# A fused two-layer cross-attention kernel: where text is scaled, where a weight is loaded, who splits what

## The chip, the cores and the metric

The kernel runs on one core of one Trainium2 chip. The metric is device time in microseconds (us) of one execution. The engines are TensorE (PE in the profile, with its weight loads as PEld), VectorE (DVE), ScalarE (ACT), GpSimd (POOL) and SyncE (SP, which here issues DMAs only). ACT issues DMAs too; in the profile SP's hardware DMA queue is q1 and ACT's is q10.

## The reference, cut to what matters

Two attention layers run one after the other on `x` (8 x 100 x 640), with the same context `ctx` (8 x 722 x 1024), of which the first 77 tokens are text and the other 645 are called ip. There are 20 heads of 32.

```
layer 1: q = x Wq.T; k,v = text Wk.T, Wv.T; k_ip,v_ip = ip Wk_ip.T, Wv_ip.T
         out = (softmax(q k /sqrt(32)) v + softmax(q k_ip /sqrt(32)) v_ip) Wo.T + bo + x
layer 2: the same with its own weights, and for the ip part
         tp    = softmax((q k_text) /sqrt(32))       # over all 640 channels at once
         sem   = ((tp text) ip.T) /sqrt(32)
         ip_p  = softmax(q_h k_ip_h /sqrt(32) + 0.5 sem) * mask
         out = (softmax(..) v + ip_p v_ip) Wout + bout + x
```

## The kernel before, in words

**Numbers.** The large products are made of float16 pairs: each operand is scaled by a power of two, rounded to float16 (the high part, on ACT) and its rest is rounded again (the low part, on DVE or POOL). A product is three matmuls per slice of the contraction (`pairs`, L510: high-high, high-low, low-high). The scale comes from the largest absolute value of the whole operand: DVE reduces each partition (`text_part` L1381, `weight_part` L1344, `context_part` L1393, `q_part` L1450), PE turns the column of 128 maxima into a row (`turn`, L530), and DVE reduces that row and makes the scale in four one-column instructions (`turned_max` L1326, `scale_chain` L1331 to L1338).

**Order.** Nothing is scheduled by a program: every engine has its own list, written out by hand, and waits on semaphores. Each layer has a prologue, and then 40 windows (8 batch rows times 5 groups of 4 heads). The prologue goes through query tiles (`q_tile`, L477, float32), the text keys (`kt_unit`, five units of 48 matmuls), the text values (`vt_unit`, five units), the ip keys of the first two groups (`k_part`), the odd tokens (`odd_unit`), and the first ip values (`v_tile`). In layer two the text logits and the semantic term of row 0 come between them. Products go to two PSUM banks in turn. A bank is free again once ACT has written the high part (L950 for keys, L961 for values) and DVE the low part (L1418, L1432).

**Text and weights in layer one.** Text lies in eight slices `k`. ACT writes the high part of each (`split_text`, L912). The even slices get their low part on DVE (`text_low`, L1387); the odd ones are first multiplied by the scale on POOL (`scale_text`, L1214) and then subtracted on POOL (`split_text`, L1220). `kt_unit(0, 0)` waits for all eight slices and for the four weight quarters, whose high parts ACT writes (`split_weight`, L900) and whose low parts DVE writes (`weight_low`, L1366).

**Buffers that tie engines to DMAs.** The high and low text keys of unit g lie in one of two buffers, and SP stores each unit with two DMAs to `k_dram` (L427). `kt_unit(l, g)` on ACT waits, for g of 2 and more, until the stores of unit g-2 have landed. It is the same with the text values (`vt_unit`, SP's L432), two buffers and one DMA each. After the last of them SP loads `sel`, stores and reloads the queries (`place_q`: L327, L330), and stores and reloads the ip keys of a group (`place_k`: L337, L341). `k_unit` (ACT L980, DVE L1507) writes the one buffer from which L337 stores, so it waits for the store of the group before. `odd_unit` on PE waits for both halves of the second `k_unit` pair.

**Weights and context in layer two.** The fourth weight (the ip values' one) comes in four quarters of 640 KB on ACT's queue (`load_weight(1, 3)`, L889), each of which waits for a low part of the third weight. The split context rows 0 and 1 are read back from `c_dram` in one DMA of 2580 KB each (`fetch_context`, L925); row 1 overwrites the buffer in which the fourth weight's quarters lie, and so waits for that weight's low parts. DVE takes the maxima of the quarters (`weight_parts`, `weight_max` L1352), and PE turns them (`weight_turn(1, 3)`) between two text value units.

**Chores in a window.** In layer one, while row i is worked on, the context of row i+1 is split during the windows of g = 1 and g = 2. POOL's part of it (`scale_context` L1227 and `split_context` L1233 of the odd slices) is hung behind its three `prob_low` instructions (L1257) per window, which PE waits for before `weigh` (L658). PE's order at the end of a window is `max_scores` of head 0 (L611), a piece of `k_part`, `weigh(u, 3)`, `max_scores` of head 1, and so on; `max_scores` of a head waits until DVE has read the row of the head before (`maxima`, L1524 and L1532).

Of the kernel before, what the change touches and what calls it, by code (L numbers as in the profile page):

```python
# [23 lines left out]
KT = CC // P  # L24
CT = C // P
# [4 lines left out]
TT = 5  # L30
# [29 lines left out]
VA = 3  # L60
ADDED = (1, 3, 5)
SLICES = (0, 2, 1, 3, 4, 6, 5, 7)

# [6 lines left out]
def xattn_pair_kernel(nc, ctx_d, text_d, x_d, w_d, wq_d, wo_d, bias_d, mask_d, const_d, sel_d, kd, qd, vd, cd, out_d):  # L70
    with ExitStack() as stack:
# [248 lines left out]
        def _(sp):  # L320
# [97 lines left out]
            sp.dma_start(x_late, x_d[1]).then_inc(x_in[1], 16)  # L418
            for s in t_low:
                sp.wait_ge(s, KT // 2)  # L420
            for h in range(2):
# [49 lines left out]
        def _(pe):  # L471
# [63 lines left out]
            def kt_unit(l, g):  # L535

                if g == 0:
                    pe.wait_ge(w_low, 16 * l + 4)
                    if l == 0:
                        for s in t_low:  # L540
                            pe.wait_ge(s, KT // 2)
                for c in range(2):
                    bank, full = bank_ready(pe, "kt", l, g, c)
                    a = ODDS + c * 4 * TEXT
                    pairs(bank[:, 0:4 * TEXT], text_weights(0, g * P, (g + 1) * P), texts(a, a + 4 * TEXT)
                          ).then_inc(full, 1)

            def vt_unit(l, t):

                if t == 0:  # L550
                    pe.wait_ge(w_low, 16 * l + 8)
                for c in range(2):
                    bank, full = bank_ready(pe, "vt", l, t, c)
                    a = ODDS + t * P
                    b = min(a + P, TW)
                    pairs(bank[0:b - a, 0:C // 2], texts(a, b), text_weights(1, c * C // 2, (c + 1) * C // 2)
                          ).then_inc(full, 1)
# [238 lines left out]
            weight_turn(0, 0)  # L796
            q_tile(0, 1, 1)
            turn(ts, t_chain, 1, "text")
            for c in range(2, CT):
                q_tile(0, 1, c)  # L800
# [44 lines left out]
            turn(qs, q_chain, 6, "q", 1)  # L845
            kt_unit(1, 4), vt_unit(1, 0), vt_unit(1, 1)
            weight_turn(1, 3)
            vt_unit(1, 2), vt_unit(1, 3), vt_unit(1, 4)
            for c in range(2):
# [31 lines left out]
        def _(act):  # L881
# [26 lines left out]
            def split_text(k):  # L908

                if k % 2:  # L910
                    act.wait_ge(t_scaled, k // 2 + 1)
                nc.scalar.activation(t_hl[:, 0, k, :], text_raw[:, k, :], ACT.Copy,  # L912
                                     scale=1.0 if k % 2 else ts[:, 4:5]).then_inc(t_high, 1)

# [238 lines left out]
            kt_unit(1, 2)  # L1153
            split_weight(1, 2, (2, 3))
            load_weight(1, 3)
            kt_unit(1, 3), kt_unit(1, 4)
            fetch_context(0)
            vt_unit(1, 0), vt_unit(1, 1)
            split_weight(1, 3, (0, 1))
            vt_unit(1, 2)  # L1160
            split_weight(1, 3, (2, 3))
            vt_unit(1, 3)
            act.wait_ge(w_low, 32)
            fetch_context(1)
            vt_unit(1, 4)
            for c in range(2):
# [3 lines left out]
            act.wait_ge(vt_out[0], 96)  # L1170
            k_unit(STEPS, 0), k_unit(STEPS, 1)
            logits(0)
            k_unit(STEPS + 1, 0), k_unit(STEPS + 1, 1)
# [12 lines left out]
        def _(pool):  # L1186
# [73 lines left out]
            def window(l, i, g):  # L1260
# [7 lines left out]
                if l == 0 and i < B - 1 and g == 1:  # L1268
                    chores = iter((lambda: (scale_context(r + 1, 3), split_context(r + 1, 1)),
                                   lambda: split_context(r + 1, 3)))  # L1270
# [23 lines left out]
            pool.wait_ge(t_chain, 5)  # L1294
            for k in range(1, KT, 2):
                scale_text(k)
            for k in range(1, KT, 2):
                split_text(k)
# [23 lines left out]
        def _(dve):  # L1322
# [427 lines left out]
            weight_scale(0, 0)  # L1750
            weight_lows(0, 0, (0, 1))
            turned_max(ts, "text")
            scale_chain(ts, t_chain, 0, ts[:, 4:5], ts[:, 5:6])
            weight_lows(0, 0, (2, 3))
            for k in range(0, KT, 2):
                text_low(k)
            weight_parts(0, 1, range(4))
            weight_max(0, 1)
            for c in range(CT):
                q_part(0, 0, c)  # L1760
            kt_unit(0, 0)
# [8 lines left out]
            weight_max(0, 2)  # L1770
            for c in range(CT):
                q_part(0, 1, c)
            q_max(0)
            kt_unit(0, 4)
            weight_scale(0, 2)
# [60 lines left out]
            kt_unit(1, 3)  # L1836
            q_scale(1)
            weight_parts(1, 3, (0, 1))
            kt_unit(1, 4)
            weight_parts(1, 3, (2, 3))  # L1840
            vt_unit(1, 0)
            weight_max(1, 3)
            weight_scale(1, 3)
            vt_unit(1, 1)
            weight_lows(1, 3, (0, 1))
            vt_unit(1, 2)
            weight_lows(1, 3, (2, 3))
            vt_unit(1, 3)
            layer_scale(1)
            vt_unit(1, 4)  # L1850
            q_split(B)
            new_scale(B)
# [73 lines left out]
```

## Time and profile before

| | us |
|---|---|
| median of 3 runs | 1921.87 (1921.60 to 1924.43) |
| the profiled execution | 1930.09 |
| its span in the profile | 1928.3 |
| PE busy | 1833.7 (95%) |
| DVE busy | 1164.6 (60%) |
| ACT busy | 781.8 (41%) |
| POOL busy | 430.7 (22%) |
| PEclk, all 40 slices | 9 tenths or more of full speed |

The span is cut into 40 slices of some 48 us. PE's busy row reads `7889999999999999998978999999999999999998`: below 9 are the prologue of layer one (slices 1 to 3), the turn to layer two and its prologue (slices 19, 21 and 22) and the end. A PE that is counted busy can still be at half its clock, since TensorE has two levels of it, 1.2 and 2.4 GHz.

### The profile page before, as it was taken

Reading aid. Unit: us, or ns where it says so; the run is one execution under the profiler, and the core shown is the slowest. Engines: PE = TensorE matmul, PEld = TensorE weight load, DVE = VectorE, ACT = ScalarE, POOL = GpSimd, SP = SyncE. Lnnn points to the kernel's source line nnn. Section 1 sums busy time; section 2 is a strip of 40 time slices with the busy share of each in tenths; the row PEclk is TensorE's granted clock in tenths of the full one; section 3 lists DMA queues with packets and bytes.
Section 4 is the critical chain, followed back from the end, with each engine's and each line's share of the span. In section 5 each row is a group of like instructions: output and inputs, shape, how many; then the busy total and the mean of one; then the engine's idle time right before and its main releaser. Section 6 shows DMA issues by size and latency. Waiting matters only on the chain.

```text
span 1928.3 us, 53974 instructions
## 1 busy us (share of the span) xinstructions
PE 1833.7 (95%) x23163; PEld 1463.6 (76%) x23163; DVE 1164.6 (60%) x2904; ACT 781.8 (41%) x1569; POOL 430.7 (22%) x522
## 2 busy tenths in 40 slices
PE   7889999999999999998978999999999999999998
PEld 4567888888888788884556788878787877878874
DVE  5776666767676767546442556566565656565653
ACT  3243454455454545442221334344343433343441
POOL 3132342423242424221000112121121112121120
PEclk9999999999999999999999999999999999999999
DMA  5753344343344343443084122323131413232221
GB/s 242 150 169 84 117 136 123 124 129 116 111 127 120 105 143 97 132 146 136 13 153 140 26 54 83 91 69 106 48 106 41 126 48 104 58 112 55 82 54 43
DMA packets 122311, 198.49 MB, mean 103 GB/s; under 512 B 40424, under 2 KB 109432, under 8 KB 115480
## 3 DMA queue, kind: packets, MB, share of 16 engines
q1 hardware_dynamic: 116600, 164.50, 30.6%
q10 hardware_dynamic: 5472, 30.54, 4.4%
q8 instruction: 183, 3.00, 0.7%
q14 instruction: 56, 0.46, 0.1%
HBM read 133.91 MB, written 60.88 MB: 101 GB/s over the span
## 4 chain that ended last, share of the span: by engine, by line
PE 77%; DVE 8%; DMA 7%; ACT 4%; issue 2%; POOL 2%; SPq 0%; ACTq 0%; POOLq 0%; DVEq 0%
PE proj L510 50%; PE pv L658 5%; PE proj L477 5%; PE rows L611 4%; PE st L634 3%; PE rows L510 3%; DMA k_dram<-arena 3%; DMA arena<-k_dram 2%; PE st L642 2%; PE rows L612 2%; ACT arena L1005 1%; DMA cbuf<-w_dram 1%; DVE wparts L1344 1%; PE rows L620 1%; DVE w_hl L1366 1%
## 5 line engine op out<-in xcount | busy, mean ns | idle before, releaser
L510 PE MATMUL proj<-w_hl,cbuf 128*128 128x128 f16 x9600 | 602.0, 219 | 0.7 <-issue 0.7
L510 PE MATMUL proj<-cbuf,w_hl 128*128 128x322 f16 (+1 forms) x3840 | 595.1, 301 | 5.0 <-DVE arena L1507 2.6
L510 PEld LDWEIGHTS proj<-w_hl,cbuf 128*128 128x128 f16 x9600 | 549.2, 98 | 7.8 <-issue 1.3
L510 PEld LDWEIGHTS proj<-cbuf,w_hl 128*128 128x128 f16 x3840 | 369.7, 97 | 171.8 <-DVE arena L1507 2.9
L1257 POOL TENSOR_TENSOR arena<-arena 128x400 f16<-128x400 f32 x240 | 235.1, 979 | 937.3 <-ACT arena L1005 937.3
L1004 ACT ACTIVATE arena<-st,rs 128x400 f16<-128x400 f32 x480 | 287.0, 598 | 373.6 <-PE st L642 159.5
L1005 ACT ACTIVATE arena<-st,rs 128x400 f32<-128x400 f32 x480 | 285.6, 595 | 0.0
L980 ACT ACTIVATE arena<-proj 128x323 f16<-128x323 f32 (+1 forms) x160 | 70.5, 442 | 502.7 <-PE proj L510 489.0
L1552 DVE TENSOR_TENSOR arena<-arena 128x400 f16<-128x400 f32 x240 | 146.2, 609 | 139.7 <-ACT arena L1005 132.0
L658 PEld LDWEIGHTS pv<-arena 128*128 128x128 f16 x4480 | 184.6, 97 | 48.2 <-POOL arena L1257 13.2
L658 PE MATMUL pv<-arena 128*128 128x66 f16 (+1 forms) x4480 | 199.0, 185 | 11.7 <-POOL arena L1257 8.2
L634 PE MATMUL st<-arena 128*128 128x100 f16 x1920 | 163.1, 207 | 0.8 <-ACT arena L1005 0.5
L1647 DVE TENSOR_TENSOR st<-st,sem_t 128x400 f32<-128x400 f32 x120 | 69.9, 582 | 152.5 <-PE st L634 152.1
L1524 DVE TENSOR_REDUCE mx<-rows 100x1 f32<-100x77 f32 x320 | 75.4, 236 | 131.1 <-PE rows L612 130.9
L611 PE MATMUL rows<-arena 96*128 96x512 f16 x320 | 122.0, 381 | 17.8 <-DVE mx L1528 11.6
L1528 DVE CUSTOM_DVE_ANT_0 raw<-rows,raw 100x645 bf16<-100x645 f32 x160 | 131.6, 822 | 0.0
L1532 DVE TENSOR_REDUCE mx<-rows 100x1 f32<-100x645 f32 x160 | 131.1, 819 | 0.0
L1507 DVE SCALAR_TENSOR_TENSOR arena<-proj,arena 128x323 f16<-128x323 f32 (+1 forms) x160 | 78.9, 494 | 75.7 <-ACT arena L980 73.3
L634 PEld LDWEIGHTS st<-arena 128*128 128x128 f16 x1920 | 114.3, 98 | 3.3 <-issue 1.2
L612 PE MATMUL rows<-arena 96*128 96x229 f16 x320 | 84.0, 263 | 0.0
L510 PE MATMUL proj<-arena,t_hl 128*128 128x320 f16 (+1 forms) x480 | 67.3, 303 | 11.3 <-DVE arena L1418 9.4
L1517 DVE SCALAR_TENSOR_TENSOR arena<-proj,arena 128x384 f16<-128x384 f32 (+1 forms) x160 | 77.2, 483 | 1.2 <-ACT arena L988 1.1
(166 smaller groups left out, 1793.8 us busy)
## 6 DMA issues: line engine op xcount, KB each, us to landing
arena<-k_dram SPq DMA_DIRECT2D x240, 185.2 KB, 3.6
k_dram<-arena SPq DMA_DIRECT2D x80, 322.5 KB, 2.9
c_dram<-cbuf SPq DMA_DIRECT2D x16, 1290.0 KB, 6.9
raw<-ctx_dram SPq DMA_DIRECT2D x14, 1290.0 KB, 7.7
cbuf<-c_dram SPq DMA_DIRECT2D x12, 1290.0 KB
cbuf<-w_dram ACTq DMA_DIRECT2D x24, 640.0 KB, 6.7
arena<-q_dram SPq DMA_DIRECT2D x48, 125.0 KB, 2.6
cbuf<-c_dram ACTq DMA_DIRECT2D x2, 2580.0 KB
```

What stands on the lines that cost most here:

```text
L477: mm = nc.tensor.matmul(bank[:, 0:MT], weight[:, c, k], src[:, k], start=(k == 0), stop=(k == CT - 1))
L510: mm = nc.tensor.matmul(out, x[a](k), w[b](k), start=(k == 0 and m == 0), stop=(k == KT - 1 and m == 2))
L611: nc.tensor.matmul(rows[:, 0, :], q, kp[0:IPO, n % 2, h, 0:512], start=True, stop=True)
L612: nc.tensor.matmul(rows[:, 1, 0:KW - 512], q, kp[0:IPO, n % 2, h, 512:KW], start=True, stop=True).then_inc(row_full, 1)
L634: mm = nc.tensor.matmul(st[:, j % 2, h * S:(h + 1) * S], kp[:, u % 2, h, a:b], qp[:, r % 2, q_col(g, h):q_col(g, h) + S], start=alone or h ...
L658: mm = nc.tensor.matmul(pv[:, part, h * VS + m * D:(h + 1) * VS], p[:, j, h * S:h * S + P], vst[:, u % 2, t, h, m * D:], start=(t < 2 and ...
L1004: nc.scalar.activation(p_hi[:, j, 0:Q4], st[:, j % 2, 0:Q4], ACT.Exp, scale=scale)
L1005: nc.scalar.activation(prob[:, j % 3, :], st[:, j % 2, 0:Q4], ACT.Exp, scale=scale).then_inc(p_high, 1)
L1257: nc.gpsimd.tensor_tensor(p_lo[:, j, 0:Q4], prob[:, j % 3, :], p_hi[:, j, 0:Q4], ALU.subtract).then_inc(p_low[1], 1)
L1528: last = nc.vector.tensor_tensor_reduce(out=junk, in0=rows_f[0:S, IPO:KW], in1=semq[r % 2], scale=1.0, scalar=LOWEST, op0=ALU.add, op1=ALU ...
L1532: last = nc.vector.tensor_reduce(mx[:, 1, h:h + 1], rows_f[0:S, IPO:KW], AX.X, ALU.max)
L1552: nc.vector.tensor_tensor(p_lo[:, j, 0:Q4], prob[:, j % 3, :], p_hi[:, j, 0:Q4], ALU.subtract).then_inc(p_low[0], 1)
```

## The change

It has five parts.

1. GpSimd takes three text slices (1, 3, 5) in place of four; slice 7 goes to DVE's `text_low`.
2. PE turns the text maxima before `q_tile(0, 1, 1)`, not behind it, and DVE makes the text scale before it writes the low parts of the first weight.
3. DVE's `q_part` of the first half moves from in front of `kt_unit(0, 0)` to in front of `kt_unit(0, 4)`, and that of the second half with `q_max` from in front of `kt_unit(0, 4)` to behind it.
4. In layer two ACT issues `load_weight(1, 3)` behind `kt_unit(1, 4)`, so that `fetch_context(0)` follows right behind it; the splits, maxima and the turn of that weight move back by one to two text value units, and `fetch_context(1)` moves behind the first `k_unit` pair.
5. POOL's first split of context in a window g = 1 has a turn of its own, behind the second `prob_low`; the next one goes behind the third.

```diff
+TEXT_POOL = (1, 3, 5)
@@ tensor
             weight_turn(0, 0)
-            q_tile(0, 1, 1)
             turn(ts, t_chain, 1, "text")
-            for c in range(2, CT):
+            for c in range(1, CT):
                 q_tile(0, 1, c)
...
-            kt_unit(1, 4), vt_unit(1, 0), vt_unit(1, 1)
+            kt_unit(1, 4), vt_unit(1, 0), vt_unit(1, 1), vt_unit(1, 2)
             weight_turn(1, 3)
-            vt_unit(1, 2), vt_unit(1, 3), vt_unit(1, 4)
+            vt_unit(1, 3), vt_unit(1, 4)
@@ scalar
             split_weight(1, 2, (2, 3))
+            kt_unit(1, 3), kt_unit(1, 4)
             load_weight(1, 3)
-            kt_unit(1, 3), kt_unit(1, 4)
             fetch_context(0)
-            vt_unit(1, 0), vt_unit(1, 1)
+            for t in range(TT - 1):
+                vt_unit(1, t)
             split_weight(1, 3, (0, 1))
-            vt_unit(1, 2)
+            vt_unit(1, 4)
             split_weight(1, 3, (2, 3))
-            vt_unit(1, 3)
-            act.wait_ge(w_low, 32)
-            fetch_context(1)
-            vt_unit(1, 4)
...
             k_unit(STEPS, 0), k_unit(STEPS, 1)
+            act.wait_ge(w_low, 32)
+            fetch_context(1)
             logits(0)
@@ gpsimd
                 if l == 0 and i < B - 1 and g == 1:
-                    chores = iter((lambda: (scale_context(r + 1, 3), split_context(r + 1, 1)),
+                    chores = iter((lambda: scale_context(r + 1, 3), lambda: split_context(r + 1, 1),
                                    lambda: split_context(r + 1, 3)))
...
-            for k in range(1, KT, 2):
+            for k in TEXT_POOL:
                 scale_text(k)
@@ vector
             weight_scale(0, 0)
-            weight_lows(0, 0, (0, 1))
             turned_max(ts, "text")
             scale_chain(ts, t_chain, 0, ts[:, 4:5], ts[:, 5:6])
-            weight_lows(0, 0, (2, 3))
-            for k in range(0, KT, 2):
-                text_low(k)
+            weight_lows(0, 0, range(4))
+            for k in range(KT):
+                if k not in TEXT_POOL:
+                    text_low(k)
             weight_parts(0, 1, range(4))
             weight_max(0, 1)
-            for c in range(CT):
-                q_part(0, 0, c)
...
             for c in range(CT):
+                q_part(0, 0, c)
+            kt_unit(0, 4)
+            for c in range(CT):
                 q_part(0, 1, c)
             q_max(0)
-            kt_unit(0, 4)
...
             q_scale(1)
+            kt_unit(1, 4)
+            vt_unit(1, 0)
+            vt_unit(1, 1)
             weight_parts(1, 3, (0, 1))
-            kt_unit(1, 4)
+            vt_unit(1, 2)
             weight_parts(1, 3, (2, 3))
-            vt_unit(1, 0)
             weight_max(1, 3)
+            vt_unit(1, 3)
             weight_scale(1, 3)
-            vt_unit(1, 1)
             weight_lows(1, 3, (0, 1))
-            vt_unit(1, 2)
-            weight_lows(1, 3, (2, 3))
-            vt_unit(1, 3)
             layer_scale(1)
             vt_unit(1, 4)
+            weight_lows(1, 3, (2, 3))
```

What ACT issues in the prologue of layer two, as a difference of the two programs (L950 are text keys, L961 text values, L900 weight splits, L889 weight loads, L925 context fetches):

```order
 L950 ACTIVATE arena<-proj 128x4x77 x2
 L900 ACTIVATE w_hl<-cbuf,wscale 128x1280 x2
+L950 ACTIVATE arena<-proj 128x4x77 x4
 L889 DMA cbuf<-w_dram 128x1280 x4
-L950 ACTIVATE arena<-proj 128x4x77 x4
 L925 DMA cbuf<-c_dram 128x10320
-L961 ACTIVATE arena<-proj 128x10x32 x4
+L961 ACTIVATE arena<-proj 128x10x32 x8
 L900 ACTIVATE w_hl<-cbuf,wscale 128x1280 x2
```

The four weight loads now stand behind the last two key units and directly ahead of the context fetch, and the first split of that weight behind four value units, not two.

DVE in the same place, in the kernel before, from the last key unit (L1418) on (L1344 are the maxima of two weight quarters, L1432 halves of value units, L1352 the weight's maximum, L1326 its turned row):

```order
L1418 SCALAR_TENSOR_TENSOR arena<-proj,arena 128x4x77
L1423 MEMSET sm 100x1
L1344 TENSOR_REDUCE wparts<-cbuf 128x1 x2
L1432 SCALAR_TENSOR_TENSOR arena<-proj,arena 128x10x32
L1435 MEMSET sm 100x1
L1432 SCALAR_TENSOR_TENSOR arena<-proj,arena 128x10x32
L1435 MEMSET sm 100x1
L1352 TENSOR_REDUCE ws<-wparts 128x1
L1326 TENSOR_REDUCE ws<-rows 128x1
```

And in the changed kernel, from the third value unit on (its numbers are one lower):

```order
L1343 TENSOR_REDUCE wparts<-cbuf 128x1 x2
L1431 SCALAR_TENSOR_TENSOR arena<-proj,arena 128x10x32
L1434 MEMSET sm 100x1
L1431 SCALAR_TENSOR_TENSOR arena<-proj,arena 128x10x32
L1434 MEMSET sm 100x1
L1343 TENSOR_REDUCE wparts<-cbuf 128x1 x2
L1351 TENSOR_REDUCE ws<-wparts 128x1
L1431 SCALAR_TENSOR_TENSOR arena<-proj,arena 128x10x32
```

The second pair of maxima and the weight's maximum stood around the first value unit; now they stand behind the third, with two halves of it ahead of them. PE's turn of that maximum, in the changed kernel:

```order
L511 MATMUL proj<-arena,t_hl 128x320 x144
L531 MATMUL rows<-const,ws 128x128
L511 MATMUL proj<-arena,t_hl 128x320 x48
L511 MATMUL proj<-arena,t_hl 104x320 x48
```

It stands behind three value units (144 matmuls), where it stood behind two (96).

## Rows read from the trace of the kernel before

**Rows 1.** The page: the chain that ended last, by engine.

```profile
PE 77%; DVE 8%; DMA 7%; ACT 4%; issue 2%; POOL 2%; SPq 0%; ACTq 0%; POOLq 0%; DVEq 0%
```

**Rows 2.** Timeline, layer one's prologue: start us, us, engine, operation [idle before <-releaser].

```profile
29.96 3.52 PE L477 MATMUL proj<-cbuf 128*128 128x400 f32 x10
...
33.32 0.27 PE L530 MATMUL rows<-const,ts 128*128 128x128 f32 x1
...
33.81 5.12 ACT L900 ACTIVATE arena<-cbuf,wscale 128x1280 f16<-128x1280 f32 x4 [3.25 <-DVE wscale L1338]
...
38.14 0.28 DVE L1326 TENSOR_REDUCE ts<-rows 128x1 f32<-128x128 f32 x1
...
39.09 4.02 DVE L1366 SCALAR_TENSOR_TENSOR arena<-cbuf,wscale,arena 128x1280 f16<-128x1280 f32 x2
...
39.26 8.67 POOL L1214 TENSOR_TENSOR raw<-raw,ts 128x656 f32<-128x656 f32 x4 [32.63 <-DVE ts L1338]
...
39.46 5.29 PE L477 MATMUL proj<-cbuf 128*128 128x400 f32 x10 [2.50 <-ACT qo L930]
...
43.04 7.57 DVE L1387 SCALAR_TENSOR_TENSOR t_hl<-raw,ts,t_hl 128x656 f16<-128x656 f32 x4
...
47.89 6.77 POOL L1220 TENSOR_TENSOR t_hl<-raw,t_hl 128x656 f16<-128x656 f32 x4
...
55.09 9.00 PE L510 MATMUL proj<-t_hl,arena 128*128 128x308 f16 x48 [5.92 <-POOL t_hl L1220]
```

**Rows 3.** Timeline, text keys and values of layer one.

```profile
86.10 2.46 DVE L1450 TENSOR_REDUCE qparts<-qo 128x1 f32<-128x400 f32 x5
...
106.33 0.32 PE L530 MATMUL rows<-const,cs 128*128 128x128 f32 x1 [1.43 <-DVE cs L1399]
```

**Rows 4.** Timeline, one window of g = 1 in layer one.

```profile
193.65 0.81 DVE L1532 TENSOR_REDUCE mx<-rows 100x1 f32<-100x645 f32 x1
...
194.11 0.39 PE L658 MATMUL pv<-arena 128*128 128x66 f16 x8 [0.72 <-POOL arena L1257]
...
194.52 0.39 PE L611 MATMUL rows<-arena 96*128 96x512 f16 x1
```

**Rows 5.** PE's waits (total us, times, longest us) over layer one's windows.

```profile
PE pv L658 <- POOL arena L1257: 5.5, 8, 0.7
```

**Rows 6.** Timeline, prologue of layer two.

```profile
973.69 6.45 PE L510 MATMUL proj<-t_hl,arena 128*128 128x308 f16 x48
...
975.73 2.86 DVE L1344 TENSOR_REDUCE wparts<-cbuf 128x1 f32<-128x1280 f32 x2
988.45 0.43 ACT L950 ACTIVATE arena<-proj 128x308 f16<-128x308 f32 x1 [14.24 <-DMA k_dram<-arena]
...
989.53 14.48 PE L510 MATMUL proj<-arena,t_hl 128*128 128x320 f16 x96 [9.39 <-DVE arena L1418]
...
1005.68 19.73 PE L510 MATMUL proj<-arena,t_hl 128*128 128x320 f16 x144 [1.55 <-DVE arena L1432]
```

**Rows 7.** Stores of text keys issued at 955.4 to 955.9.

```profile
DMA to landing us min/median/max: 7.8/7.9/8.1
```

**Rows 8.** Stores of text keys issued from 969.0 to 974.9.

```profile
DMA to landing us min/median/max: 13.8/16.6/19.4
```

**Rows 9.** DMA queues from 998 to 1000: packets, MB, share of 16 engines.

```profile
q1 hardware_dynamic: 1623, 0.31, 117.7%
q10 hardware_dynamic: 15, 0.02, 2.8%
```

**Rows 10.** Store of text values issued at 1020.0.

```profile
DMA to landing us min/median/max: 9.0/9.0/9.0
```

**Rows 11.** Store of text values issued at 1006.3.

```profile
DMA to landing us min/median/max: 2.4/2.4/2.4
```

**Rows 12.** Timeline, the end of layer two's prologue.

```profile
1041.48 0.44 ACT L980 ACTIVATE arena<-proj 128x323 f16<-128x323 f32 x1 [4.25 <-DMA k_dram<-arena]
...
1045.57 6.68 PE L510 MATMUL proj<-w_hl,t_hl 128*128 128x320 f16 x48 [1.11 <-issue]
```

More of the change, by code:

```diff
@@ L418, in _ @@
             sp.dma_start(x_late, x_d[1]).then_inc(x_in[1], 16)
-            for s in t_low:
-                sp.wait_ge(s, KT // 2)
+            for s, n in zip(t_low, (KT - len(TEXT_POOL), len(TEXT_POOL))):
+                sp.wait_ge(s, n)
             for h in range(2):
@@ L539, in kt_unit @@
                     if l == 0:
-                        for s in t_low:
-                            pe.wait_ge(s, KT // 2)
+                        pe.wait_ge(t_low[0], KT - len(TEXT_POOL))
+                        pe.wait_ge(t_low[1], len(TEXT_POOL))
                 for c in range(2):
@@ L908, in split_text @@
             def split_text(k):
-                if k % 2:
-                    act.wait_ge(t_scaled, k // 2 + 1)
+                if k in TEXT_POOL:
+                    act.wait_ge(t_scaled, TEXT_POOL.index(k) + 1)
                 nc.scalar.activation(t_hl[:, 0, k, :], text_raw[:, k, :], ACT.Copy,
-                                     scale=1.0 if k % 2 else ts[:, 4:5]).then_inc(t_high, 1)
+                                     scale=1.0 if k in TEXT_POOL else ts[:, 4:5]).then_inc(t_high, 1)
             def split_context(r, k):
@@ L1294, in _ @@
             pool.wait_ge(t_chain, 5)
-            for k in range(1, KT, 2):
+            for k in TEXT_POOL:
                 scale_text(k)
-            for k in range(1, KT, 2):
+            for k in TEXT_POOL:
                 split_text(k)
```

## Prediction

> **What bounds the kernel now.** I read the page's chain first: three quarters of the time that ends last is PE, so only what PE waits for counts, and a few microseconds each of DVE, DMA, ACT and POOL are on the chain [rows 1]. Then the timelines of the three places that the change touches, to see what ends PE's idle time there; then the DMA queues by small stretches, since two of the waits end with a DMA. The reader is to see three things.
>
> In layer one's prologue PE stands idle 5.92 before the first text key unit, which waits for POOL's last low slice, and then runs that unit at a part-time half clock, 9.00 where a unit takes 6.45 [rows 2, 6]. In the windows PE waits for POOL 5.5 in all, 0.72 of it in each of seven windows g = 1 [rows 4, 5]. In layer two's prologue PE idles 9.39: ACT has waited 14.24 for the stores of the third key unit, which took 19.4 at most where a pair alone takes 7.9 to 8.1 [rows 6 to 8]. They were in flight together with the fourth weight's quarters.
>
> **Part 1 to 3, layer one's prologue.** Before, the text maxima are turned at 33.32, but DVE reduces the turned row at 38.14, behind two weight lows, and the scale is there at 39.1 [rows 2]. DVE is free of the weight's chain at 33.8, when ACT starts its splits. The row and its four steps take 1.0 (38.14 to 39.1), so the scale comes at 34.8, 4.3 sooner. POOL then needs three scalings of 2.17 (8.67 by 4) and three subtractions of 1.69 (6.77 by 4): 34.8 + 6.5 + 5.1 = 46.4, against 54.7 before. POOL is no longer last.
>
> Late next are DVE and PE. DVE has four weight lows, of 2.01 each beside a busy POOL (4.02 by 2), from 35.1 on: 43.1 at the latest; and five text lows of 1.89 (7.57 by 4), 9.5: 52.6 as the upper bound, since after 46.4 POOL no longer slows it. PE has lost the tile that it did at 29.96, idles 3.4 until 33.6, and has four tiles to do: the first at 5.29, as before after an idle of 2.50, three at 3.52: 49.4, the lower bound. I take 50.9, near the middle. That is 4.2 before 55.09. PE has then waited 1.5. Waits of 1.11 and 1.55 left the clock full (6.68 and 19.73 / 3 = 6.58 a unit), one of 2.50 did not [rows 2, 6, 12], so the unit takes 6.45, not 9.00: 2.5 more. Gain 6.7. The q_part of the second half (2.46) now stands ahead of the third weight's scale and the first value unit on DVE; PE waits for DVE soon after anyway (1.43), and that swallows most: I take 0.6, between 0 and 2.5 [rows 3]. The key stores behind the context load have slack enough. **Sum -6.1** (bounds -8.2 and 0).
>
> A rule weighed here: the Trainium skill ("GPSIMD Engine Reference", Key points) says that GpSimd shares its SBUF interfaces with VectorE and contends with DVE instructions that have two SBUF inputs, as the lows have. The trace agrees in kind: a DVE low took 2.01 beside POOL. What it would make of the time is the rival "DVE stays late" below.
>
> **Part 5, the windows.** POOL's prob_low is no longer behind a split, so PE's wait of 0.72 goes. But the next thing PE does is the scores of head 1, at 194.52, and they wait until DVE has read the row of head 0, which ends at 193.65 + 0.81 = 194.46 [rows 4]. So PE waits there instead, and DVE's work ahead of it does not move. I take 0.03 in each of seven windows, **-0.2** (bounds 0 and 7 x 0.72 = -5.0).
>
> **Part 4, layer two's prologue.** Until the last key unit nothing moves. The stores that took 19.4 landed at 988.4 and were thus issued at 969.0; alone they land at 977. PE has the last unit's first half ready for ACT at 973.69 + 3.2 = 976.9. So the wait of 9.39 goes, and so does the slow clock behind it (14.48 for two units of 6.58, 1.3). PE runs on from 980.1 with three value units: 999.9.
>
> There two new waits stand. First, the turn of the weight's maximum now needs DVE's second pair of maxima, which DVE does behind the third value unit: an estimated 1.1 for that unit's last eviction (ACT's half took 0.43), 2.86 for the pair, 0.2 for the maximum: 4.2 [rows 6]. Second, the third value unit on ACT needs the store of the first unit to have landed. That store is queued on SP behind the last key stores (issued 981). The weight and the context, 5.1 MB, now start at the same moment on ACT's queue. Before, the context went out at 988.5 and the last key stores soon behind it; from 998 to 1000 q10 ends (15 packets) and q1 starts in earnest (1623) [rows 9]: the small packets had waited for the large ones. 2.6 MB thus took 10.2 with its start, and I take 6.4 for a second such load right behind: the bulk ends at 981 + 16.6 = 997.6. The key pair alone would take 7.9, the value store 2.4 [rows 7, 11]; part of the 7.9 is start and landing, so I take 6.4 for both: landed at 1004 (bounds 997, before anyone waits, and 1012 with 10.2, 10.2, 7.9 and 2.4 in full). ACT and DVE then do the unit (1.5), the maxima and the turn (3.4): PE resumes at 1008.9, after an idle of 9, runs two units in 13.2 + 1.3, and is done at 1023.4. Before it was done at 1005.68 + 19.73 = 1025.4 [rows 6]. **Sum -2.0**: of the 10.7 removed, 8.7 come back (bounds -6.5 and +5.7).
>
> A rule weighed here: the Trainium skill ("DMA: Bandwidth & Descriptors", Queues, rings and completion order) says that an engine turns round between the queue rows packet by packet, and that a semaphore's increment lands only after every earlier write of that DMA engine, over all its queues. The rows show the first (small packets starve beside large ones); by the second a small store could not report before the loads ahead of it, which is the rival "the queue holds longer".
>
> Then the second context fetch. It used to go out during the fourth value unit; a store of values beside it took 9.0, alone 2.4: 6.6 more [rows 10, 11]. Now it goes out an estimated 8.7 behind the value units' end E, when ACT has evicted the first k_part pair, beside the reload of the queries and the ip key store of group 0, for which ACT already waited 4.25, until E + 16.1 [rows 12]. The last value store no longer shares with a fetch; I take it 0.9 sooner, so I start from E + 15.2, add the 6.6, and 1.4 for both evictions of the second group: the odd unit starts at E + 23.2, where it was E + 20.2 (1045.57), and PE, idle for 6 by then, is slow again (1.3). **Sum +4.3** (bounds -2.2, when nothing is held up and PE's own matmuls set it, and +9).
>
> **The sum.** -6.1 - 0.2 - 2.0 + 4.3 = -4.0. The profiled execution took 1930.09 (span 1928.3), 8.2 above the median of the runs, and would be 1926.1; the median of 1921.87 becomes 1917.9.
>
> **The rivals.**
> *One or both DMA waits don't come.* For it: ACT's and SP's packets do share the engines, and the stores of the queries are out before the fetch. Against it: rows 9 and 10. Without the value store's wait PE resumes at 1004.4, not 1008.9: 4.5 less, 1913.4. Without the fetch's 6.5 less, 1911.4. Without both 1906.9.
> *The queue holds longer (slower).* SP's small packets get nothing until ACT's loads have ended. The store lands at 1012, PE's units end 7.7 later than forecast, and the query store is caught too, up to 2.4 + 0.6 more: 1917.9 + 7.7 + 3 = 1928.6, or 1925.6 without the latter. It decides from a landing at 1009 on. For it: the 19.4 of rows 8. Against it: the two loads are one stream and pay their start once.
> *DVE stays late.* The lows all cost their price beside POOL: keys start at 52.6, PE has idled 3.2 and is slow (9.00). Part 1 to 3 gives 2.5 - 0.6 = 1.9, not 6.1: 1922.1. For it: the rule above; against it POOL ends 6 sooner.
> *The chores pay in full*, since DVE's reads move with POOL's: 4.8 more, 1913.1. Against it the 0.06 between 194.46 and 194.52.
>
> **How the numbers follow.** Forecast 0.42 (its own range 1914.5 to 1921), one or both DMA waits missing 0.27 (both 0.05), the queue longer 0.15, DVE late 0.11, chores 0.05. What a measurement can tell from no change is 0.2%, 3.8: below 1918.0 is faster, above 1925.7 slower. The forecast lies on that edge: 0.24 of it faster, 0.18 the same. Faster 0.24 + 0.27 + 0.05 = 0.56; same 0.18 + 0.11 + 0.03 = 0.32; slower 0.12. The range leaves out the case of both waits missing and the slower end, 0.17 in all: 1909 to 1924.5.
>
> **What would show it.** Right: keys of layer one start at 50 to 52 and the first unit takes 6.5; `proj<-arena,t_hl` of layer two starts at once behind the keys; after its third unit PE is idle for some 9, with ACT waiting for `v_dram`; ACT's second `k_unit` pair waits for `k_dram` longer than 4.25; in the windows g = 1 PE's wait on POOL is gone and its scores wait for DVE. Wrong: an idle of only 4.5 behind the third value unit, an odd unit at less than E + 20, or windows g = 1 shorter by 0.7.

## The result and the profile after

| | before | after |
|---|---|---|
| median of 22 executions each, us | 1925.56 | 1932.2 |
| lowest to highest, us | 1921.6 to 1933.23 | 1925.51 to 1938.23 |
| profiled execution (span), us | 1930.09 (1928.3) | 1931.96 (1930.1) |
| ratio, 95% interval | | 1.0037 (1.0028 to 1.0046) |

The change makes the kernel slower, by 0.37%: 7.1 us, between 5.4 and 8.9. The forecast was 4 us faster, and it gave "slower" a chance of 0.12. Two executions, the profiled one of `e1_old_chores` below and one of the kernel before in the same session, ran at granted clocks of 0.58 and 0.56 and took over 3000 us; no ratio here counts them.

The two profiled spans differ by 1.8 only. The stretches below say where the change costs; behind the last of them, from the turn of layer two's first probabilities to the end, the traces take 875.4 before and 870.9 after, and between 870.7 and 876.3 in the other kernels, so that no difference there can be put down to the change.

The chain of the page, by engine, after: POOL has gone from 2% to none, ACT from 4% to 2%, DVE from 8% to 9% [rows 1].

```profile
PE 78%; DVE 9%; DMA 7%; issue 3%; ACT 2%; SPq 0%; ACTq 0%; POOL 0%; POOLq 0%; DVEq 0%
```

The timeline of layer one's prologue after (start us, us, engine, operation, idle before and its releaser), against [rows 2]:

```profile
33.02 0.29 PE L531 MATMUL rows<-const,ts 128*128 128x128 f32 x1 [2.73 <-DVE ws L1325]
33.15 15.36 PE L478 MATMUL proj<-cbuf 128*128 128x400 f32 x40
51.42 6.44 PE L511 MATMUL proj<-t_hl,arena 128*128 128x308 f16 x48 [2.91 <-DVE t_hl L1386]
```

The keys start 3.7 sooner, wait for DVE and no longer for POOL, and run at full clock. So far the forecast holds. The same window g = 1 as in [rows 4], after:

```profile
183.18 1.26 POOL L1226 TENSOR_TENSOR raw<-raw,csb 128x645 f32<-128x645 f32 x1
185.09 0.95 POOL L1256 TENSOR_TENSOR arena<-arena 128x400 f16<-128x400 f32 x1 [0.65 <-ACT arena L1005]
185.26 1.46 DVE L1408 SCALAR_TENSOR_TENSOR cbuf<-raw,csb,cbuf 128x645 f16<-128x645 f32 x1
185.99 2.00 POOL L1232 TENSOR_TENSOR cbuf<-raw,cbuf 128x645 f16<-128x645 f32 x1
186.78 1.64 DVE L1551 TENSOR_TENSOR arena<-arena 128x400 f16<-128x400 f32 x1
188.83 0.81 DVE L1531 TENSOR_REDUCE mx<-rows 100x1 f32<-100x645 f32 x1
189.70 0.39 PE L612 MATMUL rows<-arena 96*128 96x512 f16 x1 [1.51 <-DVE mx L1531]
```

PE's wait of 0.72 for POOL has become one of 1.51 for DVE. The same rows of before show why:

```profile
190.67 0.88 DVE L1409 SCALAR_TENSOR_TENSOR cbuf<-raw,csb,cbuf 128x645 f16<-128x645 f32 x1
191.27 1.54 POOL L1233 TENSOR_TENSOR cbuf<-raw,cbuf 128x645 f16<-128x645 f32 x1 [1.43 <-ACT cbuf L919]
192.20 1.05 DVE L1552 TENSOR_TENSOR arena<-arena 128x400 f16<-128x400 f32 x1 [0.65 <-ACT arena L1005]
```

DVE's low part of the context takes 1.46 after and 0.88 before, its low part of the probabilities 1.64 and 1.05. The first 0.58 costs nothing here: before, DVE waited 0.65 for ACT between the two, and the second begins 1.52 behind the start of the first after and 1.53 before. The other 0.59 reaches PE. POOL's split runs beside the first 1.2 of that instruction; before, it was 0.6. From one turn of the maxima to the next, this window took 20.02 before and takes 20.60. PE's waits over layer one's windows, after (total us, times, longest), against [rows 5]:

```profile
PE rows L612 <- DVE mx L1531: 11.4, 8, 1.5
```

Layer two's prologue after, against [rows 6, 12]:

```profile
982.24 19.72 PE L511 MATMUL proj<-arena,t_hl 128*128 128x320 f16 x144
...
1005.55 0.77 ACT L961 ACTIVATE arena<-proj 128x320 f16<-128x320 f32 x2 [9.63 <-DMA v_dram<-arena]
...
1010.28 0.47 PE L531 MATMUL rows<-const,ws 128*128 128x128 f32 x1 [8.32 <-DVE ws L1351]
1010.55 16.00 PE L511 MATMUL proj<-arena,t_hl 128*128 128x320 f16 x96
...
1048.62 0.77 ACT L980 ACTIVATE arena<-proj 128x323 f16<-128x323 f32 x2 [10.62 <-DMA k_dram<-arena]
1050.09 8.48 PE L511 MATMUL proj<-w_hl,t_hl 128*128 128x320 f16 x48 [6.52 <-issue]
```

The stop behind the keys is gone and two new ones stand where they were forecast. From the start of layer two's keys (946.99, now 949.26) to the turn of the first probabilities (1052.91, now 1059.23), the stretch is 4.05 longer.

### The profile page after: what moved, and what is told of

The parts are those of the page before. It is cut to its first block, busy times and chain, and to the rows that moved or that the text cites. A ratio compares the mean times of both kernels' runs of the same rounds, so it can differ in the third digit from the quotient of the medians.

```text
span 1930.1 us, 53973 instructions
## 1 busy us (share of the span) xinstructions
PE 1828.7 (95%) x23163; PEld 1461.6 (76%) x23163; DVE 1174.6 (61%) x2905; ACT 781.3 (40%) x1569; POOL 431.6 (22%) x520
## 4 chain that ended last, share of the span: by engine, by line
PE 78%; DVE 9%; DMA 7%; issue 3%; ACT 2%; SPq 0%; ACTq 0%; POOL 0%; POOLq 0%; DVEq 0%
PE proj L511 51%; PE pv L659 5%; PE proj L478 5%; PE rows L612 4%; PE st L635 4%; DMA arena<-k_dram 3%; PE rows L511 3%; PE st L643 2%; DMA k_dram<-arena 2%; PE rows L613 2%; DMA v_dram<-arena 1%; ACT arena L1005 1%; DVE wparts L1343 1%; DMA cbuf<-w_dram 1%; DVE arena L1365 1%
## 5 line engine op out<-in xcount | busy, mean ns | idle before, releaser
L1551 DVE TENSOR_TENSOR arena<-arena 128x400 f16<-128x400 f32 x240 | 150.4, 626 | 135.3 <-ACT arena L1005 127.4
L988 ACT ACTIVATE arena<-proj 128x384 f16<-128x384 f32 (+1 forms) x160 | 70.8, 442 | 10.1 <-PE proj L511 10.1
```

The source lines that it names most:

```text
L1551: nc.vector.tensor_tensor(p_lo[:, j, 0:Q4], prob[:, j % 3, :], p_hi[:, j, 0:Q4], ALU.subtract).then_inc(p_low[0], 1)
```

## The experiments

My theory, T, is that three terms add up: the start gains, the spread chores cost because POOL's work now overlaps DVE's, and layer two's prologue costs by two late stores. The rivals are named with each run. A ratio is to the kernel before, with its 95% interval; microseconds are the ratio, or a difference of two, times 1925.5, and a difference of two carries some 3 us of doubt either way (3.7 for `e9_best` against the changed kernel, 4.6 for `e10_low_later` against `e9_best`).

**The parts by themselves.** `e1_old_chores` is the changed kernel with:

```diff
-  chores = iter((lambda: scale_context(r + 1, 3), lambda: split_context(r + 1, 1),
+  chores = iter((lambda: (scale_context(r + 1, 3), split_context(r + 1, 1)),
```

> The changed kernel with the windows' context chores as they were (part 5 undone), the rest kept. Theory T, the spread chores cost time: in the trace of the changed kernel each of the seven windows g = 1 of layer one is 0.59 longer than before, because GpSimd's split and low part now run beside VectorE's low parts and slow them (VectorE's context low 1.46 where it took 0.88, its low part of the probabilities 1.64 where it took 1.05), and TensorE's scores of head 0 wait 1.51 for VectorE's maxima. So this kernel is 7 x 0.59 = 4.1 us faster than the changed one and stands at a ratio of about 1.0015 to before. Rival C, the loss is TensorE's slow clock and later context transfers and the chores are free: the same ratio as the changed kernel, about 1.0037.

Measured: 1.0019 (1.0005 to 1.0033), 3.5 us below the changed kernel. T's figure lies in it, the rival's 1.0037 does not; but the two kernels' intervals overlap, and the next run is the firmer one. None of its rows is used. It is still 3.7 us slower than before (1.0 to 6.4): the change loses without part 5 too.

`e2_chores_only` is the kernel before with the opposite edit.

> The kernel before with nothing but the spread chores. Theory T: each of seven windows g = 1 is 0.6 longer, TensorE no longer waits for GpSimd but for VectorE's maxima, and the kernel is 4.1 us slower, ratio 1.002. Rival C: no difference that can be measured, 1.000. The blind forecast gave this part -0.2 us.

Measured: 1.0025 (1.0014 to 1.0035), 4.8 us. The same window takes 20.59, and the trace shows the wait that the changed kernel has; PE's waits in layer one's windows:

```profile
PE rows L611 <- DVE mx L1532: 11.4, 8, 1.5
```

So part 5 alone makes the windows longer, in the kernel before as in the changed one. The rival falls.

`e3_start_only` is the changed kernel with parts 4 and 5 undone.

> The kernel before with the first three parts alone (text slices 1, 3, 5 on GpSimd, the text scale ahead of the weight lows, q_part of layer one later). Theory T: what is gained ahead of the windows stays: 5.4 to 6 us faster, ratio 0.997. Rival: a start that is 6 us earlier against the same transfers is given back in the windows (TensorE's waits for the rows from DRAM were 1.9 us longer in the changed kernel): 0.998 to 1.000.

Measured: 0.998 (0.9969 to 0.9991), 3.9 us faster. The windows give nothing back that can be seen: TensorE turns a window's maxima at 162.91 before and 3.95 sooner here, and the layer's last ones at 874.01 before and 3.76 sooner here. But less is gained than T said, and the timeline shows where:

```profile
32.98 0.29 PE L531 MATMUL rows<-const,ts 128*128 128x128 f32 x1 [3.70 <-DVE ws L1326]
33.13 13.67 PE L478 MATMUL proj<-cbuf 128*128 128x400 f32 x40
51.38 8.11 PE L511 MATMUL proj<-t_hl,arena 128*128 128x308 f16 x48 [4.57 <-DVE t_hl L1387]
```

The query tiles took 13.67 here and 15.36 in the changed kernel, so PE was done sooner, idled 4.57 and not 2.91, and its key unit took 8.11 and not 6.44. The same 2.91 was not always followed by the faster unit, though: in `e7_fetch1_late`, `e9_best` and `e10_low_later`, with tiles of 15.36 as well, the unit took 7.82 to 8.11:

```profile
51.63 8.11 PE L511 MATMUL proj<-t_hl,arena 128*128 128x308 f16 x48 [2.91 <-DVE t_hl L1386]
```

DVE sets the start of the keys, 51.4 in both.

`e4_load_only` is the kernel before with part 4 alone.

> The kernel before with the fourth part alone (layer two's prologue: the fourth weight's load behind the text keys, the second context fetch behind the first k_part pair, the new order on VectorE). Theory T: TensorE's stop behind the keys goes, one of 8 to 9 us comes behind the third value unit, and the second fetch costs 6 us at the odd unit: net +4, ratio 1.002. Rival, the loss there is a matter of one execution's clock: -2 us as forecast for the first half, up to -6, ratio 0.997 to 0.999.

Measured: 1.0027 (1.0014 to 1.004), 5.2 us. The rival falls. The timeline of layer two's prologue has the same stops as the changed kernel:

```profile
1013.35 0.48 PE L530 MATMUL rows<-const,ws 128*128 128x128 f32 x1 [8.38 <-DVE ws L1351]
...
1051.67 9.36 PE L510 MATMUL proj<-w_hl,t_hl 128*128 128x320 f16 x48 [6.57 <-issue]
```

-3.9 + 4.8 + 5.2 = 6.1: this lies within the interval of the measured 7.1 (5.4 to 8.9).

**The chores' price.** `e5_splits_last` is the changed kernel with:

```diff
-  chores = iter((lambda: scale_context(r + 1, 3), lambda: split_context(r + 1, 1),
-                 lambda: split_context(r + 1, 3)))
+  chores = iter((lambda: scale_context(r + 1, 3), lambda: None,
+                 lambda: (split_context(r + 1, 1), split_context(r + 1, 3))))
```

> The changed kernel with both context splits of a window g = 1 (slices 1 and 3) behind GpSimd's third low part of the probabilities; nothing stands between its low parts but the one scaling. Theory T, what makes the windows longer is the overlap of GpSimd's split with VectorE's low parts: with the split gone from there the window loses the 0.59 and the 0.72 of before as well, 7 x 1.3 = 9 us faster than the changed kernel, ratio to before 0.999. Rival O, it is an order effect (TensorE now waits for VectorE's maxima whatever GpSimd does): at most the 4.1 us come back, ratio 1.0015 or more.

Measured: 1.0004 (0.9992 to 1.0016), 6.4 us below the changed kernel: between the rival's 4.1 and T's 9, and the time alone excludes neither. The window does: it takes 19.68, less than the 20.02 of before, to which the rival would have brought it back. Its timeline, DVE's low part, POOL's two splits and PE's scores:

```profile
186.98 0.58 DVE L1551 TENSOR_TENSOR arena<-arena 128x400 f16<-128x400 f32 x1
...
188.83 0.39 PE L612 MATMUL rows<-arena 96*128 96x512 f16 x1 [0.45 <-DVE mx L1531]
...
189.17 2.79 POOL L1232 TENSOR_TENSOR cbuf<-raw,cbuf 128x645 f16<-128x645 f32 x2
```

Alone, DVE's low part takes 0.58 instead of 1.64. A wait of 0.45 stays, which I had not counted.

`e6_small_split` is the changed kernel with:

```diff
+  w = 8 if r > 1 and k == 1 else IP
-  nc.gpsimd.tensor_tensor(c_part(r % 2, 1)[:, k, :], ctx_raw[:, k, :], c_part(r % 2, 0)[:, k, :],
+  nc.gpsimd.tensor_tensor(c_part(r % 2, 1)[:, k, 0:w], ctx_raw[:, k, 0:w], c_part(r % 2, 0)[:, k, 0:w],
```

> The changed kernel with GpSimd's split of context slice 1 cut to 8 of its 645 columns in six of the seven windows g = 1 (the other columns of that low part keep what an earlier context left there). Order, waits and semaphores are as in the changed kernel. Theory T, contention: VectorE's third low part of the probabilities goes back from 1.64 to 1.05 or less, TensorE's scores wait less for the maxima, and each of the six windows is about 0.6 to 1.3 shorter: 4 to 8 us faster than the changed kernel, ratio 0.9995 to 1.0015. Rival O, order: VectorE's instructions keep their lengths, nothing changes, 1.0037.

Measured: 1.001 (0.9998 to 1.0021), 5.2 us below the changed kernel. The timeline of a window with the small split:

```profile
277.08 1.46 DVE L1409 SCALAR_TENSOR_TENSOR cbuf<-raw,csb,cbuf 128x645 f16<-128x645 f32 x1
277.80 0.79 POOL L1233 TENSOR_TENSOR cbuf<-raw,cbuf 128x8 f16<-128x8 f32 x1
278.60 0.57 DVE L1552 TENSOR_TENSOR arena<-arena 128x400 f16<-128x400 f32 x1
...
280.45 0.39 PE L612 MATMUL rows<-arena 96*128 96x512 f16 x1 [0.45 <-DVE mx L1532]
```

The order is that of the changed kernel, instruction by instruction; only the data that POOL moves is less. DVE's low part of the probabilities shrinks from 1.64 to 0.57 and the window from 19.36 to 18.29. It is the split still running beside it, and not the order. DVE's low part of the context still takes 1.46, so that one is not what lengthens the window.

**The two late stores.** `e7_fetch1_late` is the changed kernel with:

```diff
-  act.wait_ge(w_low, 32)
-  fetch_context(1)
   logits(0)
   k_unit(STEPS + 1, 0), k_unit(STEPS + 1, 1)
   odd_unit(1)
+  act.wait_ge(w_low, 32)
+  fetch_context(1)
```

> The changed kernel with the second context fetch of layer two moved behind the odd unit on ScalarE. Theory T, the small key store of group 0 starves beside the fetch: ScalarE's wait for k_dram of 10.6 falls to 4.3 or less, TensorE's 6.5 idle before the odd unit to about 1, and its slow clock behind goes too: 6 to 8 us faster than the changed kernel, ratio 0.9995 to 1.0005. Rival: the store waits for something else on its queue (the reload of queries ahead of it): under 2 us, 1.003 or more.

Measured: 1.0002 (0.9991 to 1.0013), 6.7 us below the changed kernel. The store of group 0 (bytes, median us from issue to landing), first in the changed kernel, then here:

```profile
k_dram<-arena SPq DMA_DIRECT2D x1, 322.5 KB, 9.2
```

```profile
k_dram<-arena SPq DMA_DIRECT2D x1, 322.5 KB, 2.9
```

And the timeline, where ACT waits 4.35 and PE 1.11, as before [rows 12]:

```profile
1040.45 0.44 ACT L980 ACTIVATE arena<-proj 128x323 f16<-128x323 f32 x1 [4.35 <-DMA k_dram<-arena]
1042.78 6.68 PE L511 MATMUL proj<-w_hl,t_hl 128*128 128x320 f16 x48 [1.11 <-issue]
```

`e8_fetch0_early` is the changed kernel with `fetch_context(0)` moved from behind `load_weight(1, 3)` to behind the query tiles `q_tile(1, 1, c)`.

> The changed kernel with the first context fetch of layer two issued behind the last query tiles, 35 us earlier, so that the fourth weight loads alone. Theory T, two things end TensorE's 8.3 idle behind the third value unit: the value store that lands late beside 5.1 MB of loads, and VectorE's second pair of maxima, which stands behind that unit. The first goes, the second leaves an idle of 4.3: 4 us faster than the changed kernel, ratio 1.0015 to 1.002. Rival Q, the fetch now holds up the first key stores instead and TensorE stops among the key units: 0 to 5 us slower than the changed kernel, 1.004 to 1.006.

Measured: 1.0012 (1.0001 to 1.0024), 4.8 us below the changed kernel. The timeline shows an idle of 4.16, where T had worked out 4.3, and no stop among the keys, so rival Q falls:

```profile
995.58 0.44 ACT L961 ACTIVATE arena<-proj 128x320 f16<-128x320 f32 x1 [3.90 <-DMA v_dram<-arena]
1001.89 0.47 PE L531 MATMUL rows<-const,ws 128*128 128x128 f32 x1 [4.16 <-DVE ws L1351]
```

`e12_early_maxima` takes the other half. It is the changed kernel with, on DVE:

```diff
   vt_unit(1, 0)
-  vt_unit(1, 1)
   weight_parts(1, 3, (0, 1))
-  vt_unit(1, 2)
+  vt_unit(1, 1)
   weight_parts(1, 3, (2, 3))
   weight_max(1, 3)
+  vt_unit(1, 2)
   vt_unit(1, 3)
```

> The changed kernel with VectorE's two pairs of maxima of the fourth weight behind its value units 0 and 1, the third and fourth unit behind them; both fetches as in the changed kernel. Theory T, the idle of 8.3 has two parts in a row, 4 for the value store that lands late and 4 for the maxima behind it: the second goes, 4 us faster than the changed kernel, ratio 1.0015 to 1.002, the idle 4.2. Rival: the maxima then wait for the weight itself, which lands late beside the context (they were at 996.5 in the changed kernel): under 2 us.

Measured: 1.0021 (1.0006 to 1.0036), 3.1 us below the changed kernel, with 3.4 of doubt: the time does not tell T's 4 from the rival's 2, but the timeline does. The turn comes at once, and PE idles 3.67 for the bank that waits on the store:

```profile
1003.45 0.27 PE L531 MATMUL rows<-const,ws 128*128 128x128 f32 x1
1007.40 14.89 PE L511 MATMUL proj<-arena,t_hl 128*128 128x320 f16 x96 [3.67 <-DVE arena L1431]
```

The idle of 8.3 is, but for 0.5, the two in a row, 4.16 and 3.67, as forecast.

**The slices.** `e11_four_slices` is `e3_start_only` with `TEXT_POOL = (1, 3, 5, 7)`.

> The kernel before with the first three parts, but with four text slices on GpSimd again (1, 3, 5, 7). Theory T: the scale ahead of the weight lows makes the gain, the three slices none: VectorE's lows are done about 1.3 us sooner, GpSimd's at 50, the keys of layer one start at 50 to 51 (51.4 with three), 0 to 1.5 us faster than with three slices, ratio 0.997 to 0.998. Rival: GpSimd is last again as before, keys at 53 or later and the first unit in slow clock: 0.9985 or more.

Measured: 0.9991 (0.998 to 1.0003), where three slices gave 0.998; the intervals overlap, but the timeline speaks against T (the view ends inside the key unit, which takes 9.14 in all):

```profile
43.41 8.62 POOL L1220 TENSOR_TENSOR t_hl<-raw,t_hl 128x656 f16<-128x656 f32 x4
44.71 8.02 DVE L1387 SCALAR_TENSOR_TENSOR t_hl<-raw,ts,t_hl 128x656 f16<-128x656 f32 x4
52.83 7.44 PE L511 MATMUL proj<-t_hl,arena 128*128 128x308 f16 x35 [4.27 <-DVE t_hl L1387]
```

Four slices on DVE take 8.02, five took 6.48: 2.0 against 1.3 each, because POOL subtracts beside them to the end. With one slice more on POOL, DVE is 1.5 later. POOL ends at 52.03 and DVE at 52.7, so the rival has the slow unit right, the keys nearly so, and the engine wrong. Taking the fourth slice off POOL is worth having, for DVE's sake; the scale ahead makes the rest (52.8 against 55.1).

**A better version.** `e9_best` has the edits of `e5`, `e7`, `e8` and `e12` together in the changed kernel.

> The changed kernel with four edits together: both context splits of windows g = 1 behind GpSimd's third low part; the first context fetch of layer two behind the last query tiles; the second one behind the odd unit; VectorE's two pairs of maxima of the fourth weight behind its value units 0 and 1. Theory T: of the four costs found each goes, 6.4 us in the windows, 6.7 at the odd unit, 4.8 and another 4 behind the third value unit (TensorE's idle there under 1): 22 us below the changed kernel, ratio to before 0.992. Rival G, gains are given back at the next wait (key stores beside the early fetch, windows of layer two): 0.996 or more.

Measured over 6 executions: 0.9927 (0.991 to 0.9944), 1910.77 us: 14 us below before and 21 below the changed kernel, where T said 22. The rival falls. The timeline: PE runs through from the keys to the end of the value units:

```profile
975.96 19.72 PE L511 MATMUL proj<-arena,t_hl 128*128 128x320 f16 x144
995.52 0.27 PE L531 MATMUL rows<-const,ws 128*128 128x128 f32 x1
995.63 13.20 PE L511 MATMUL proj<-arena,t_hl 128*128 128x320 f16 x96
...
1027.08 6.68 PE L511 MATMUL proj<-w_hl,t_hl 128*128 128x320 f16 x48 [1.11 <-issue]
```

`e10_low_later` is the same with DVE's lows of the context spread otherwise:

```diff
-  lows = iter((4 * (g - 1), 4 * (g - 1) + 2) if l == 0 and i < B - 1 and g in (1, 2) else ())
+  lows = iter({1: (0,), 2: (2, 4, 6)}.get(g, ()) if l == 0 and i < B - 1 else ())
   if l == 0 and g == 2 and i < B - 1:
+      low()
       new_scale(r + 1)
```

> The kernel with the four edits, and VectorE's low part of context slice 2 moved from window g = 1 to the start of window g = 2. Theory T: TensorE's rest wait of 0.45 for VectorE's maxima in each window g = 1 goes, and g = 2 has room (VectorE is idle 1.94 there): 7 x 0.45 = 3 us faster than with the four edits alone, 0.9985 of it. Rival: the 0.9 to 1.6 that it takes at the start of window g = 2 delays the first low parts there and costs as much: no difference, or slower.

Measured over 7 executions: 0.9961 (0.9945 to 0.9978), 6.5 us slower than the version above. PE's waits in layer one's windows:

```profile
PE pv L659 <- DVE arena L1551: 9.0, 7, 1.3
...
PE rows L612 <- DVE mx L1531: 3.9, 8, 0.9
```

The wait for the maxima is the same 3.9, and that for DVE's first low part is 9.0 where the version above has 3.0: 6.0 more, nearly all of the loss. The low that I moved had stood in time in which DVE waited for ACT's high part anyway. T was wrong here, the rival right.

## Why the prediction was wrong

**Part 5** is the step that failed most: "DVE's work ahead of it does not move." Forecast -0.2 (bounds -5.0 and 0), measured +4.8 (`e2_chores_only`). I had seen that PE would wait for DVE next, and took DVE's instructions at the lengths that they had beside POOL's old order. The new order puts POOL's low part on DVE's low of the context, which costs nothing since DVE had 0.65 to spare behind it, and more of POOL's split on DVE's low of the probabilities. That one is 0.59 longer, in place of the 0.72 that PE waited there is 1.51, and the window is 0.58 longer; seven such windows are 4.1 of the 4.8. I had used the very rule in layer one's prologue: the Trainium skill ("GPSIMD Engine Reference", Key points) has GpSimd share its SBUF interfaces with VectorE and contend with DVE instructions that have two SBUF inputs. DVE's low of the probabilities is one, and the runs agree with the rule: 0.57 alone, 1.64 beside a split. My bounds for this term were below zero on one side only; nothing in the rows excluded a loss.

It is the largest error, 5.0 of the 10.1 us between the forecast's sum and that of the runs, but it does not decide the sign alone: with part 5 undone the kernel is still 3.7 us slower than before (`e1_old_chores`). The other two steps had their mechanisms right and their sizes wrong.

**Parts 1 to 3** were forecast at -6.1 (bounds -8.2 and 0) and gave -3.9 (`e3_start_only`, 1.7 to 6.0 faster). The step was right and 2.2 too large, within that doubt; in the changed kernel's own trace the first turn of a window's maxima comes 5.4 sooner (157.50, was 162.91). Keys at 50.9, measured 51.4: DVE's four weight lows took 9.85 and not 8.0, its five text lows 6.48 and not 9.5. The 2.01 for a weight low was the mean of two unlike ones: the 4.02 of rows 2 is one of 1.53, which began before POOL did, and one of 2.57 beside POOL. In the new order all four are beside POOL. What was too sure is the term of 2.5 for the full clock: the unit took 6.44 in the changed kernel and in four others with waits of 1.7 to 1.9, 7.8 to 8.1 in three with the changed kernel's wait of 2.91, and 8.11 behind 4.57. The 0.6 for q_part no run takes apart.

**Part 4** went as told. The stop behind the keys went. PE resumed after 8.3, forecast 9; the turn waited for the late maxima (4.16 when alone, forecast 4.2) and the value store (3.67 when alone, forecast 4.5 more than the maxima). The odd unit came 23.5 behind the value units, forecast 23.2, by a store that took 9.2 beside the fetch. But +2.3 was forecast and +5.2 measured (`e4_load_only`, 2.7 to 7.7). The mis-sized term is the 10.7 that the change takes away. Its 9.39 of idle came from one row [rows 6], and three other kernels that keep this prologue as it was stop there for less, here `e3_start_only` and `e2_chores_only`:

```profile
982.41 15.43 PE L511 MATMUL proj<-arena,t_hl 128*128 128x320 f16 x96 [5.01 <-DVE arena L1418]
```

```profile
993.33 15.25 PE L510 MATMUL proj<-arena,t_hl 128*128 128x320 f16 x96 [7.87 <-DVE arena L1418]
```

In `e11_four_slices` it is 5.88. From the start of layer two's keys to the turn of the first probabilities these three take 101.0, 103.3 and 100.9, the kernel before 105.9; the four with part 4 as in the changed kernel take 109.3 to 110.0. So the 4.05 above is one pair out of differences that run from 3.4 to 9.1; between the means it is 6.9. Why the stop varies stays open: ACT waited 14.24 for the store before and 9.86 and 12.72 in the two shown. The rest is slow clock: in the changed kernel the two value units took 16.00 where I had 14.5, and the odd unit 8.48 where I had 8.0. The 1.3 that I took for each restart came from one row too [rows 6]; the same two units took 14.48 in `e4_load_only`, behind an idle as long (8.38).

**The rivals.** None is what happened. The one on the slower side, the queue that holds longer, needed a landing from 1009 on; ACT had its store at 1005.5. Both DMA waits came. "DVE stays late" had keys at 52.6; they came at 51.4, though its slow first unit came in five of the kernels with the scale ahead. "The chores pay in full" had the right place and the wrong sign. Summed by the runs: -3.9 + 4.8 + 5.2 = 6.1, where I had -6.1 - 0.2 + 2.3 = -4.0.

## What to carry to other kernels

When a chore moves on GpSimd, write down what VectorE does in that time, before and after, and price VectorE's two-input instructions anew if VectorE is what TensorE waits for next; a wait removed on the one engine can be paid on the other. A small store that someone waits for, and a bulk load that nobody needs yet, belong in different stretches: two loads, one issued 35 us earlier and the other some 17 us later, took 4.8 and 6.7 us off, and with the maxima ahead some 15 in all. Before a wait is priced by one row, look whether the same wait has the same length in another kernel: the stop that part 4 removes was 9.4 in one trace and 5.0 to 7.9 in three others. And an edit that fills a gap of an engine is worth nothing when the gap is there because the engine waits, and costs where it is taken from (`e10_low_later`).

## What was not expected of the hardware

TensorE's clock after one and the same idle. At the turn of the layers PE waits 2.77 for ACT and then does a query tile of ten matmuls. In the kernel before and two of the others (the changed kernel and the fourth part alone):

```profile
908.78 3.62 PE L477 MATMUL proj<-extra,cbuf 128*128 128x400 f32 x10 [2.77 <-ACT qo L930]
```

```profile
909.36 5.32 PE L478 MATMUL proj<-extra,cbuf 128*128 128x400 f32 x10 [2.78 <-ACT qo L930]
```

```profile
911.00 6.70 PE L477 MATMUL proj<-extra,cbuf 128*128 128x400 f32 x10 [2.77 <-ACT qo L930]
```

The granted clock over the tile was 1.00, 0.68 and 0.54: the level of 2.4 GHz in the first, of 1.2 GHz for nearly the whole tile in the last, and for part of it in the second. Of the thirteen traces other than that of `e1_old_chores`, seven have 3.6, four 5.1 to 5.3, two 6.7. The idle and the instructions are the same, and no row shows what decides. So a profile of one execution can be up to 3 us off at each such place, and a forecast should not take a restart's cost from one row.

GpSimd is slowed as well: its split of 645 columns took 2.00 beside DVE's low part and 1.41 alone. Read to the end of each instruction, the windows look as if GpSimd and VectorE's low parts took turns, a whole instruction at a time. In the changed kernel DVE's low of the probabilities starts beside the split and ends 0.43 behind its end (188.42 and 187.99); in the same window of the kernel before it is 193.25 and 192.81. In all thirteen traces 253 of the 255 low parts of the probabilities that began beside a running GpSimd instruction end 0.43 to 0.45 behind it, and those that did not begin beside one take 0.55 to 0.58. It holds the other way round: the split ends 1.27 behind DVE's low of the context (187.99 and 186.72), and the split of 8 columns, which took 0.79, ends 0.05 behind it (278.59 and 278.54). DVE's maxima, which read one tensor, took 0.81 to 0.82 beside GpSimd and without. So what such an instruction costs hangs on which engine began first, and on how long that one still has to run.

What stays open: PE's waits for the rows of the keys from DRAM in layer one's windows, 4.6 before and 6.3 after, were between 2.5 and 5.1 in the other kernels (without `e1_old_chores`), in no order that I can name. Up to 2 us of the changed kernel's loss in its trace may lie there; no run takes this wait apart.
